# Decoder on one core: position matrices by register-addressed transfers, and group norms moved into the attention's last bodies

## What is computed

```python
x = x + _L0_attn_ref(_layernorm(x), ...)            # self attention        ("A")
x = x + _L0_xattn_ref(_layernorm(x), ctx_1024, ...) # local cross attention ("B")
x = x + _L0_ffn_ref(_layernorm(x), ...)             # recurrence, 32 steps  ("C")
x = x + _L1_attn_ref(_layernorm(x), ...)            # relative attention    ("P")
x = x + _L1_xattn_ref(_layernorm(x), itok, ctx_1024)# position matrices     ("E")
x = x + _L1_ffn_ref(_layernorm(x), ...)             # routed experts        ("F")

def _L1_xattn_ref(x, layer_idx, weight):            # E: weight is ctx_1024, 32 x 128 x 128
    w = weight[layer_idx]                           # 128 matrices, one a position, chosen among 32
    return jnp.einsum('bsd,sod->bso', x, w)         # each multiplies the 32 batch rows of its position
```

## Time and profile before

| | us |
|---|---|
| median of 3 runs (1407.62 to 1413.79) | 1409.27 |
| the profiled execution, device time | 1406.79 |
| its span, first to last instruction | 1405.0 |
| PE, DVE, ACT, POOL busy in the span | 1131.8, 1002.9, 843.0, 563.6 |
| relative attention, first position scores written to last residual | 790.8 to 1098.9 |
| group norms of E, to the first multiplication | 1098.9 to 1124.8 |
| multiplications of E, to the last one's end | 1124.8 to 1150.4 |
| way through DRAM and first sum | 1150.4 to 1157.1 |
| first norm, gate and routing of the experts, then the experts | 1157.1 to 1405.0 |

### The profile page before, as it was taken

How to read it: one execution, slowest core, us unless ns; L and a number is a source line. 1 busy time by engine, 2 the same in 40 slices (tenths; PEclk the granted TensorE clock), 3 DMA queues, 4 the chain that set the end, 5 groups by cost and what they waited for, 6 DMA issues and landing times. The chain is left out here.

```text
span 1405.0 us, 40905 instructions
## 1 busy us (share of the span) xinstructions
PE 1131.8 (81%) x12518; PEld 741.7 (53%) x12567; DVE 1002.9 (71%) x3715; ACT 843.0 (60%) x1689; POOL 563.6 (40%) x794
## 2 busy tenths in 40 slices
PE   2787888786598898898598788888888437999998
PEld 1344445454355555555386466666666234666665
DVE  2688888884466666666465388999998728888885
ACT  1577787885377777777233488888886333333231
POOL 4777777770222222222010266666665421211120
PEclk9999999999699999999899899999999567999999
DMA  5000000000000000000000388888888130000000
GB/s 174 1 2 1 0 0 0 0 2 1 1 2 2 0 0 0 0 0 1 1 0 1 90 222 235 233 234 233 233 236 222 45 101 21 8 12 12 7 8 15
DMA packets 152048, 82.89 MB, mean 59 GB/s; under 512 B 6875, under 2 KB 150373, under 8 KB 151701
## 3 DMA queue, kind: packets, MB, share of 16 engines
q1 hardware_dynamic: 151428, 79.65, 20.8%
q0 software_dynamic: 528, 2.10, 0.5%
HBM read 43.72 MB, written 38.01 MB: 58 GB/s over the span
## 5 line engine op out<-in xcount | busy, mean ns | idle before, releaser
L765 POOL TENSOR_TENSOR rr<-ms_eps,minus_half 128x16 f32<-128x16 f32 x64 | 185.2, 2912 | 11.6 <-DVE ms_eps L980 11.6
L507 PE MATMUL psum<-identb,stacks 128*128 128x128 bf16 x1800 | 137.7, 224 | 35.7 <-DVE stacks L1029 12.6
L1114 DVE TENSOR_REDUCE rowmax<-psum 128x4 f32<-128x768 f32 x128 | 123.0, 961 | 60.1 <-PE psum L2082 60.1
L507 PEld LDWEIGHTS psum<-identb,stacks 128*128 128x128 bf16 x1800 | 110.8, 100 | 66.6 <-issue 24.2
L1315 DVE CUSTOM_DVE_ANT_0 summed<-psum,pos_score 128x128 f32<-128x128 f32 x512 | 118.0, 285 | 23.2 <-PE psum L2282 15.3
L1882 ACT ACTIVATE pos_rows<-psum 128x512 f32<-128x512 f32 x72 | 43.0, 597 | 142.0 <-PE psum L2458 129.9
L2324 PE MATMUL psum<-consts,summed 128*128 128x128 f32 x512 | 82.7, 285 | 38.6 <-DVE summed L1321 36.9
L1019 DVE TENSOR_REDUCE rowmax<-psum 128x4 f32<-128x512 f32 x128 | 84.9, 686 | 34.4 <-PE psum L1948 34.4
L1767 ACT ACTIVATE probsT<-psum 128x512 f32<-128x512 f32 x128 | 77.0, 601 | 51.9 <-PE psum L598 34.8
L598 PE MATMUL psum<-probsT,values 128*32 128x128 f32 x2048 | 85.0, 282 | 26.9 <-DVE attn L624 22.5
L372 POOL TENSOR_TENSOR rstd<-vareps,minus_half 128x4 f32 (+1 forms) x24 | 25.3, 1055 | 196.0 <-DVE vareps L363 196.0
(11 more groups left out here) (270 smaller groups left out, 3053.7 us busy)
## 6 DMA issues: line engine op xcount, KB each, us to landing
skew<-pos_rows SPq DMA_DIRECT2D x128, 258.0 KB, 3.8
pos_score<-skew SPq DMA_DIRECT2D x128, 256.0 KB, 4.1
X<-in_x_dram POOLq DMA_DIRECT2D x1, 2048.0 KB, 11.6
ctxT<-in_ctx_dram SPq DMA_DIRECT2D x1, 2048.0 KB, 9.9
out_dram<-X SPq DMA_DIRECT2D x8, 256.0 KB, 2.3
w_up<-in_L_ffn_w_e_dram SPq DMA_DIRECT2D x2, 512.0 KB, 3.8
y_rows<-hidden SPq DMA_DIRECT2D x4, 256.0 KB, 2.3
y_rows<-qT SPq DMA_DIRECT2D x4, 256.0 KB, 2.3
```

The source lines that it names most:

```text
L507: last = pe.transpose(turned[:, t, :], stacks[:, which, 2 * t:2 * t + 2, :].rearrange("s h k -> s (h k)"), identb[:, :])
L765: pool.tensor_tensor(out=rr[:, par, i * H:(i + 1) * H], in0=ms_eps[:, i * H:(i + 1) * H], in1=minus_half[:, 0:H], op=ALU.pow).then_inc(A.r ...
L1114: dve.tensor_reduce(rowmax[:, par, PT * r:PT * r + PT].rearrange("s (h b) -> s b h", b=2), B.max_space, AX.X, ALU.max, negate=True).then_i ...
```

## The change

Copies inside SBUF are gone. SP brings each of the 128 matrices from DRAM by a transfer whose source address holds a register, loaded from `itok`. The destinations: 32 into `yT` once A is done; 32 into `ctxT` itself and 39 into 13 tensors that nothing uses any more, once B is done; these are the 103 of `EARLY`. The last 25 go to `pos_rows`, behind the last `read_shifted`; their 25 layer numbers are loaded into registers ahead of the attention and kept. `y_chunk` takes half of `kT` where it had `qT`.

The group norms move into the last four bodies of the attention, as their batches are done. DVE keeps the statistics, POOL takes power and application for groups 0 to 6, and every group has its own buffer (`xn_spaces`); two PSUM banks take turns. Group 7 stays behind the attention. Groups 0 to 3 are saved to the second half of `seqT`, the others to the first, and the way back through DRAM follows (`slot`).

The weights of the experts are loaded at the start of the program, `spread` behind B; its cast stands ahead of the attention on DVE.

```diff
+        EARLY = 103
+        dead_rows = [wblk[:, :, :, :].rearrange("s a h d -> s (a h d)"), k3T[:, :, :].rearrange("s a k -> s (a k)"),
...
+        late_rows = pos_rows[:, :, :, :].rearrange("s a h k -> s (a h k)")
...
+        def chosen_layer(eng, chunk, j):
+            return eng.value_load(itok[0:1, 16 * chunk + j:16 * chunk + j + 1], min_val=0, max_val=NB - 1)
+
+        def fetch(eng, chunk, j, layer, sem):
+            eng.dma_start(matrix(chunk, j), t["ctx_1024"][:, at(layer), :].rearrange("d a o -> d (a o)")).then_inc(sem, 16)
+
+        def stats_in_tail(dve, g):
+            n = E.base + g
+            wait(dve, P.x, 4 * g + 4)
...
+        def rstd_in_tail(pool, g):
+            wait(pool, E.var, E.base + g + 1)
+            pool.tensor_tensor(out=rstd4[:, 4 * g:4 * g + 4], in0=vareps4[:, 4 * g:4 * g + 4], in1=minus_half[:, 0:4], op=ALU.pow).then_inc(E.rstd, 1)
+
+        def apply_in_tail(eng, g):
+            wait(eng, E.rstd, E.base + g + 1)
+            for k in range(4):
+                last = eng.tensor_scalar(E.xn_spaces[g][:, k:k + 1, :], X[:, 4 * g + k:4 * g + k + 1, :], meanvar8[:, g, k, 0:1],
+                                         rstd4[:, 4 * g + k:4 * g + k + 1], ALU.subtract, ALU.mult)
+            last.then_inc(E.xn, 1)
```

SP, ahead of the relative attention:

```diff
+            sp.wait_ge(ld.e, 16)
+            sp.wait_ge(A.x, NB)
+            for chunk in (2, 3):
+                for j in range(16):
+                    fetch(sp, chunk, j, chosen_layer(sp, chunk, j), E.early)
+            sp.wait_ge(B.x, NB)
+            sp.dma_start(spread[:, :, :], t["spread"].rearrange("k (t m) -> k t m", t=TILES - 1)).then_inc(ld.f, 16)
+            for i in [*range(NB), *range(2 * NB, EARLY)]:
+                fetch(sp, i // 16, i % 16, chosen_layer(sp, i // 16, i % 16), E.early)
+            late_layers = {i: chosen_layer(sp, i // 16, i % 16) for i in range(EARLY, S)}
```

SP, behind the last `read_shifted`:

```diff
+            for i in range(EARLY, S):
+                fetch(sp, i // 16, i % 16, late_layers[i], E.late6 if i < 7 * 16 else E.late7)
```

POOL, behind its attention work:

```diff
-                pool.wait_ge(P.x, NB)
                 for g in range(NB // 4):
-                    ln_group_rstd(pool, E, g)
-                    for j in (2 * g, 2 * g + 1):
-                        gather_one(pool, pool.tensor_copy, j // 8, j % 8, E.by_pool)
-                for chunk in (4, 5, 6, 7):
-                    gather_chunk(pool, pool.tensor_copy, "pool", chunk, E.by_pool)
+                    rstd_in_tail(pool, g)
+                    if g < NB // 4 - 1:
+                        apply_in_tail(pool, g)
```

DVE in an attention body, behind `take_max(b, 1)`, and then behind `add_max` of the next batch's quarter 1:

```diff
+                    if left == 3:
+                        stats_in_tail(dve, 0)
+                        stats_in_tail(dve, 1)
+                    if left == 2:
+                        stats_in_tail(dve, 2)
+                        stats_in_tail(dve, 3)
+                    if left == 1:
+                        stats_in_tail(dve, 4)
...
+                    if left == 1:
+                        stats_in_tail(dve, 5)
+                        stats_in_tail(dve, 6)
```

PE in an attention body, behind the scores of quarter 3, and then behind `turn_less(b, 3)`:

```diff
+                    if left == 1:
+                        turn_in_tail(pe, 0)
+                    if left == 0:
+                        turn_in_tail(pe, 1)
...
+                    if left == 0:
+                        turn_in_tail(pe, 2)
```

PE, at the head of a chunk of `multiply`:

```diff
-                    wait(pe, E.by_pool, gathered_until("pool", chunk))
-                    wait(pe, E.by_dve, gathered_until("dve", chunk))
-                    wait(pe, E.by_act, gathered_until("act", chunk))
+                    wait(pe, E.early, 16 * EARLY)
+                    if chunk == 6:
+                        wait(pe, E.late6, 16 * (7 * 16 - EARLY))
+                    if chunk == 7:
+                        wait(pe, E.late7, 16 * 16)
```

More of the change, by code:

```diff
@@ L397, in matrix, with in_group_slots @@
-        def matrix(chunk, j):
[L398 to L412, removed]
+        def in_group_slots(g):
+            return (g + NB // 8) % (NB // 4)
@@ new lines, in decoder @@
+        dead_places = [rows[:, i * D:(i + 1) * D] for rows, n in zip(dead_rows, (4, 4, 3, 3, 2, 8, 8, 1, 1, 1, 1, 2, 1)) for i in range(n)]
+        late_rows = pos_rows[:, :, :, :].rearrange("s a h k -> s (a h k)")
+        assert len(dead_places) == EARLY - 2 * NB
+        def matrix(chunk, j):
+            i = 16 * chunk + j
+            if i < NB:
+                return ctxT[:, i, :]
+            if i < 2 * NB:
+                return yT[:, i - NB, :]
+            if i < EARLY:
+                return dead_places[i - 2 * NB]
+            return late_rows[:, (i - EARLY) * D:(i - EARLY + 1) * D]
@@ new lines, in chosen_layer @@
+        def chosen_layer(eng, chunk, j):
[5 more added lines that the diff above has]
+            wait(dve, P.x, 4 * g + 4)
+            wait(dve, E.aggr, n)
+            for k in range(4):
+                last = dve.bn_stats(stats4[:, k, :], X[:, 4 * g + k, :])
+            last.then_inc(E.stats, 1)
+            wait(dve, E.stats, n + 1)
+            wait(dve, E.var, n)
+            dve.memset(carrier[0:1, :], 0.0)
+            for k in range(4):
+                last = dve.bn_aggr(meanvar8[:, g, k, :], stats4[:, k, :])
+            last.then_inc(E.aggr, 1)
+            wait(dve, E.aggr, n + 1)
+            dve.tensor_scalar(vareps4[:, 4 * g:4 * g + 4].unsqueeze(2), meanvar8[:, g, :, 1:2], LN_EPS, None, ALU.add).then_inc(E.var, 1)
@@ new lines, in turn_in_tail, with save_in_tail @@
+        def turn_in_tail(pe, g):
+            wait(pe, E.xn, E.base + g + 1)
+            wait(pe, E.xnT, E.base + g - 1)
+            for k in range(4):
+                last = pe.transpose(E.ln_banks[g % 2][:, k * S:(k + 1) * S], E.xn_spaces[g][:, k, :], ident)
+            last.then_inc(E.xnT_ps, 1)
+        def save_in_tail(act, g):
+            slot = in_group_slots(g)
+            wait(act, E.xnT_ps, E.base + g + 1)
+            if g >= NB // 8:
+                wait(act, P.s, (NB - 3 + g - NB // 8) * R)
+            act.activation(seqT[:, 4 * slot:4 * slot + 4, :], E.ln_banks[g % 2].rearrange("d (b s) -> d b s", b=4), ACT.Copy).then_inc(E.xnT, 1)
@@ L730, in _ @@
             for i in range(4):
[L731 removed]
+                first, last = BACK[i]
                 sp.dma_start(yT[:, 4 * first:4 * last, :], y_rows[:, 4 * first:4 * last, :]).then_inc(E.back[i], 16)
@@ L1342, in body @@
                         ln_apply(dve, P, b + 4, b + 4)
+                dve.wait_ge(ld.f, LOADS_F)
+                dve.wait_ge(F.zeroed, 2)
+                dve.tensor_copy(spreadb[0:3 * EX, :, :], spread[:, :, :]).then_inc(F.cast, 1)
                 residual_h(0, 0)
@@ L1840, in position_weights @@
             def position_weights():
[L1841 to L1848 removed]
+                for g in range(4, NB // 4):
+                    save_in_tail(act, g)
                 def save_y(i):
```

104 lines of the change are left out of this document (40 added, 64 removed).

## The result

The changed kernel takes 1386.51 us, median of 4 runs (1384.77 to 1389.26), against 1411.53 (1407.62 to 1416.54, 4 runs) before. The measured ratio is 0.9837, with a 95% interval of 0.981 to 0.9864; the quotient of the two medians is 0.9823, inside it. Run again beside three of the experiments it gave 1385.59 us and 0.984 (0.9816 to 0.9864). The forecast was 1387.

A forecast was written before the change was run, and what follows sets the result against it. Bound by norms (25.9 us) and waits for gathered copies (9.2) behind the attention; attention's end 11 later, group 7 6.2, multiplications 12.3: 22.1 less than 1406.79, 1384.7, plus 2.5 for the median, 1387 us; range 1377 to 1400.

The forecast's parts named there:

- 6 us of stretch with 9.8 of multiplications: Low end of the range, given as 1377 us: least delay of the attention's end, with the multiplications' lower bound.
- Statistics, 8.1 us: Attention bodies 28 to 30: seven groups' statistics on DVE, 1.78 us each, less hidden waits, add 8.1 us.
- clock, 1.4: Attention's last bodies: half clock on PE behind the statistics' two pauses costs 1.4 us, bounds 0 and 7.
- PE's turns, 1.5 us: Attention's last bodies: group 2's turn on PE puts 1.1 us on the path, group 3's 0.4.
- POOL beside DVE, at nothing: Attention's last four bodies: POOL's work slowing DVE's subtractions counted as nothing; by the skill's rule about 1.7 us more.
- POOL's applications at 0.59: Attention's tail: one application takes POOL 0.59 us, a group 3.5, seven 24, so groups 5 and 6 are ready in time.
- The rival of POOL as the bound: Attention's tail: applications of 2 us bring the whole to about 1411 us, of 1.3 to 1394; chance 0.08.
- SP, 0.81 to 1.11 a fetch: Ahead of the attention: SP's register loads and transfers end between 751.8 and 780.6 us, hidden before its 790.80 start.
- Group 7, 6.2 us: Behind the attention: group 7's statistics, power, application, turn and save take 6.2 us to the first multiplication.
- Multiplications, 12.3 us: Behind group 7: three chunks at 2.06 us and five at 1.22, no waits on copies; bounds 9.8 and 16.5.
- one of the signs that I had named: In the multiplications: chunks waiting for a transfer or for a save would show the forecast wrong.
- Nothing behind the first sum: Behind the multiplications: the save, the way through DRAM, all behind it and the experts' clock stay as they were.

The follow-up runs named there:

- the first two experiments: Changed kernel with the norms back behind the attention: 1397.66 us; changed kernel with 96 of the matrices copied by engines, norms in the tail: 1402.82 us.
- the kernel with statistics alone: Changed kernel with powers, applications, turns and saves of all groups behind the last residual, only statistics in the attention's tail: 1414.56 us, one run.
- the norms alone: Changed kernel with norms kept in the attention's tail, but 96 matrices copied by POOL, DVE and ACT behind the attention: 1402.82 us, ratio 0.9941.
- the last kernel: Changed kernel with PE's pauses in the last four attention bodies filled with turns of the identity, nothing else: 1385.36 us, ratio 0.9846.
- all fillers and saves apart: Changed kernel with identity turns filling PE's pauses in four bodies and around group 7's turn, DVE saving every second chunk: 1388.01 us, ratio 0.9846.

## Why the prediction was right, step by step

The two halves, their sizes and the end of the sum came as reasoned, and the first two experiments show the halves apart. Several terms were off and partly cancel. That 1387 came within 1.5 us of both medians is in part luck: in the profiles the gain was 2.8 us less than the sum, and the profiled run of the changed kernel lies 1 us above its median, where that of before lies below. One slip stands in the range: 6 us of stretch with 9.8 of multiplications add up to 1379.5, not 1377.

- **Statistics, 8.1 us, and clock, 1.4.** The sum of the stretch was right (11 against 9.1 and 10.3), its split is open. A group is 1.44 us, not 1.78, as nothing waits inside it here; DMA's waits vanished as foreseen. With the clock held at 1.00 the tail is 42.8, 4.2 above before, and without it 47.8 and 49.0: the lower clock is worth 5 to 6 us there, near my upper bound of 7. But the kernel before has half-clock spells too: over the tail its granted clock is 0.87, that of the changed kernel 0.79 and 0.82. By these shares it is at half clock for some 10 us before and 17 to 21 after, an estimate, so perhaps half of the 5 to 6 is new. 4.2 is the least that the statistics add. The kernel before with its own pauses filled, which would settle the split, was not run.
- **PE's turns, 1.5 us.** Without them and without the applications the tail was 49.4. They cost nothing that shows, within the 3 us that a profile can tell.
- **POOL beside DVE, at nothing.** Right. In the changed kernel DVE's eight subtractions beside POOL took 0.698 us on average, while POOL's application took 0.94 in one group; with DVE idle it takes 0.797, as this group of rows of the kernel with statistics alone shows, ahead of one of the changed kernel:

```profile
L439 POOL TENSOR_SCALAR hidden<-X,meanvar,rstd 128x128 f32<-128x128 f32 x8 | 6.3, 797 | 0.2
```

```profile
L439 POOL TENSOR_SCALAR wx<-X,meanvar,rstd 128x128 f32<-128x128 f32 x4 | 3.7, 941 | 0.1
```

  Here POOL was the one that lost time, off the path. The Trainium skill, SBUF — State Buffer, section "SBUF: two separate sides", lets the later of the two wait. In this trace that is so behind POOL's casts, as in the earlier trace rows: 26 subtractions of the changed kernel that began behind one took 0.97 to 0.98 us. It is not so behind the applications: seven that began inside one took 0.68 to 0.74, and the 1.7 us that I drew from the rule did not come.
- **POOL's applications at 0.59.** Too low: 0.79 or more, a group 4.2 to 4.8 us instead of 3.5, group 6 ready at 1108.3, less than 4 us ahead of its turn at 1112.13. The rival of POOL as the bound was nearer than its 0.08 said (its 1394 for 1.3 us is 1392 by the sum that gave the 1411).
- **SP, 0.81 to 1.11 a fetch.** 1.105, the upper end; the loads end at 778.3, inside 751.8 to 780.6. A second load adds 0.56. The Trainium skill, DMA: Bandwidth & Descriptors, section "Latency and other measured facts", has some 0.6 as the floor of a register load; the trace is near it, with 0.56 for each of the 25 loads alone.
- **Group 7, 6.2 us.** 5.65 and 5.18.
- **Multiplications, 12.3 us.** From the first start to the last one's end 11.7 and 11.1, to the last save's end 12.4 and 12.2. The chunks went from half clock to 1.22 us each as reasoned, and with every chunk at the higher clock the end came at 10.1, near my bound of 9.8. Two things I had not seen: a chunk waits up to 0.2 us for a save, one of the signs that I had named, and an earlier end of the multiplications doesn't bring the experts' first sum forward, as the last write lands later.
- **Nothing behind the first sum.** Here the changed kernel gives 2.4 us back, against the one profile of before that there is. DVE's timeline, then PE's, in the middle of the experts:

```profile
1272.42 0.69 DVE L1539 TENSOR_TENSOR X<-X,psum 128x512 f32 x1 [2.99 <-issue]
...
1274.67 1.32 PE L2538 MATMUL psum<-w_down,pos_rows 128*128 128x128 f32 x8 [1.73 <-DVE pos_rows L1532]
```

  DVE stands still for 2.99 us with no releaser, PE pauses for 1.73, and the granted clock is 0.50 from 1276 to 1278. Before, DVE's longest such gap in that stage is 1.58. The gap of 3 us stands at the same place, 138 to 141 us behind the first sum, in all other profiles but one, that of the norms alone. Packets of a queue that the profile calls "instruction" fall into it and none into the same stretch of before; that DVE's code arrives late there is argued, not shown. Nor is the gap all of it: the kernel with the norms alone takes 250.8 us for that stage without it.

The profiled pair differs by 19.3 us, the sum had 22.1; what lacks stands in the first and last rows of the table, 4.5 us, against which the three rows between them gave 1.7 more than the sum. The medians differ by more, 23 to 25, since the profiled run of before was about 4 us below the median of its later 25 runs, 1410.81, where I had reckoned with 2.5.

What stays open: fillers shorten the tail by up to 6 us in the profiles, yet no median shows it beyond its interval (1381 to 1392 from run to run in the last kernel, with clocks of 0.954 to 0.964 over the span). The two profiles with the shortest tails are of the fastest of six runs each, so the tails of the slower runs are not known. A version that is surely faster than the changed kernel was not found.

## What to carry to other kernels

Work moved into the body of another loop is to be priced with the pause that it makes on the engine that waits: here the added DVE work cost at least 4 us, and the half clock in the same bodies up to 6. A cover is worth measuring in the queue that uses it: SP had 15.5 us left, and one more register load per transfer would have eaten the whole gain. A stage that ends in a transfer is priced together with it: at the higher clock the products were ready 1.5 us sooner, and the last write to DRAM landed so much later that at most 0.3 us were left.

## What was not expected of the hardware

A save of 128x512 from PSUM takes 0.64 to 0.66 us in the kernel before and 0.99 to 1.04 in the changed one (groups of ACT, before, then after; mean ns of one):

```profile
L1853 ACT ACTIVATE qT<-psum 128x512 f32<-128x512 f32 x4 | 2.6, 644 | 2.1 <-PE psum L2430 2.1
```

```profile
L1903 ACT ACTIVATE kT<-psum 128x512 f32<-128x512 f32 x4 | 4.1, 1038 | 1.0 <-PE psum L2485 1.0
```

With all fillers and saves apart, the timeline of ACT, SP and DVE:

```profile
1111.68 1.00 ACT L1915 ACTIVATE hidden<-psum 128x512 f32<-128x512 f32 x1 [1.39 <-PE psum L2499]
1112.63 1.06 DVE L1445 COPY hidden<-psum 128x512 f32<-128x512 f32 x1 [3.69 <-PE psum L2499]
1112.71 1.39 SPq L789 DMA_DIRECT2D y_rows<-hidden  x2
...
1120.53 0.69 DVE L1445 COPY kT<-psum 128x512 f32<-128x512 f32 x1 [1.42 <-PE psum L2499]
```

The first save is slow with no write to DRAM under way, the last one fast while writes run; PE multiplies into the other bank during the first and is done at the last. So it seems to be PE's products at the higher clock that slow the saves, on ACT and on DVE alike; over all profiles a save beside products takes 0.60 to 0.84 at a granted clock of 0.50 and 0.74 to 1.38 at 1.00, and with PE done 0.6 on ACT and 0.69 on DVE at either. In the steady attention a 128x512 exponential beside a busy PE takes 0.60, so it isn't PE's work as such. What it is in these products was not tried.
